# Joining paired operations across two PSUM banks in a fused attention and feed-forward kernel

## The reference

```
q, k, v = split(x @ Wqkv)                  # 16 heads of 64
q = l2norm(q) * qs; k = l2norm(k) * ks     # then a rotary embedding with scales
sim  = 8 * q k^T  in windows of 32 tokens, each looking at itself and the one before
sim  = where(mask, -max, sim)
attn = softmax(sim)
x    = x + (attn @ v) @ Wo
x    = x + (a * gelu(gate)) @ W2 + b2,   a, gate = split(layernorm(x) @ W1 + b1)
```

## Time and profile before

| | |
|---|---|
| time, median of 3 runs | 1455.85 us (1452.92 to 1457.2) |
| profiled execution, its own time | 1451.59 us |
| its span, first to last instruction | 1449.7 us |
| busy: PE matmul, PE weight load | 1357.1 us (94%), 1094.5 us (75%) |
| busy: DVE, ACT, POOL | 1294.6 (89%), 1266.6 (87%), 1184.0 us (82%) |
| chain that ended last, by engine | PE 47%, DVE 19%, issue 15%, ACT 6%, POOL 5% |
| a turn of the loop, around 740 us | 28.14 us |
| granted clock, mean | 0.986 |

### The profile page before, as it was taken

One profiled execution on the slowest core, in us unless ns is written; L12 is line 12 of the kernel. 1 busy time (PEld: TensorE's weight loads), 2 busy tenths in 40 slices (PEclk: granted clock), 3 DMA queues, 4 the chain that ended last, 5 costly groups with the idle time before them and its releaser, 6 DMA issues.

```text
span 1449.7 us, 76627 instructions
## 1 busy us (share of the span) xinstructions
PE 1357.1 (94%) x30176; PEld 1094.5 (75%) x30176; DVE 1294.6 (89%) x2400; ACT 1266.6 (87%) x2523; POOL 1184.0 (82%) x1162
## 2 busy tenths in 40 slices
PE   6589999999999999999999999999999999999985
PEld 4467777877777777777777777777777778777774
DVE  6688999999999999999999999999999999999973
ACT  6578999999999999999999999999999999899873
POOL 2687888888888888888888888888888888888860
PEclk9899999999999999999999999999999999999998
DMA  5221112131111222111122111113111112111111
GB/s 148 81 57 41 38 48 57 36 89 42 51 39 47 57 57 68 42 50 39 47 70 61 50 43 50 39 46 95 36 43 36 36 37 77 43 29 43 43 31 30
DMA packets 61752, 75.09 MB, mean 52 GB/s; under 512 B 8462, under 2 KB 35340, under 8 KB 61708
## 3 DMA queue, kind: packets, MB, share of 16 engines
q1 hardware_dynamic: 61708, 74.51, 18.8%
HBM read 18.90 MB, written 1.05 MB: 14 GB/s over the span
## 4 chain that ended last, share of the span: by engine, by line
PE 47%; DVE 19%; issue 15%; ACT 6%; POOL 5%; DVEq 2%; ACTq 0%; POOLq 0%
PE bank L1275 12%; PE bank L1178 6%; PE bank L1266 6%; DVE ss L906 5%; PE bank L1191 5%; PE bank L1179 4%; PE bank L1180 4%; DVE psum L943 4%; POOL u L444 3%; DVE u L913 3%; PE bank L1228 3%; PE bank L1311 3%; DVE t L922 3%; PE bank L1300 2%; ACT gate L714 2%
## 5 line engine op out<-in xcount | busy, mean ns | idle before, releaser
L444 POOL TENSOR_TENSOR u<-u,t 128x512 f32<-128x512 f32 x384 | 490.5, 1283 | 84.3 <-DVE t L922 68.5
L457 POOL TENSOR_TENSOR u<-u,rn 128x512 f32<-128x512 f32 x384 | 388.9, 1045 | 0.0
L628 ACT ACTIVATE sq<-bank 128x512 f32<-128x512 f32 x384 | 234.0, 610 | 64.0 <-PE bank L1180 62.0
L1178 PE MATMUL bank<-Wl,xsh 128*128 (+1 forms) x576 | 268.0, 465 | 15.4 <-POOL xsl L439 11.3
L463 POOL TENSOR_TENSOR P<-P,rs 128x512 f32<-128x512 f32 x192 | 196.6, 1045 | 95.0 <-DVE rs L948 95.0
L922 DVE TENSOR_TENSOR t<-bank,TS 128x512 f32<-128x512 f32 x384 | 258.7, 684 | 6.1 <-ACT sq L628 2.1
L906 DVE TENSOR_REDUCE ss<-sq 128x8 f32<-128x512 f32 x384 | 255.6, 676 | 6.4 <-issue 6.4
L913 DVE TENSOR_TENSOR u<-bank,TC 128x512 f32<-128x512 f32 x384 | 255.1, 675 | 1.3 <-ACT sq L628 1.3
L652 ACT COPY qkT<-bank 128x512 f32<-128x512 f32 x384 | 225.2, 603 | 13.5 <-PE bank L1191 6.4
L1179 PE MATMUL bank<-Wh,xsl 128*128 (+1 forms) x576 | 228.8, 397 | 0.0
L1180 PE MATMUL bank<-Wh,xsh 128*128 (+1 forms) x576 | 228.7, 397 | 0.0
(11 more groups left out here) (92 smaller groups left out, 2732.1 us busy)
## 6 DMA issues: line engine op xcount, KB each, us to landing
vs<-v SPq DMA_DIRECT2D x384, 128.0 KB, 2.3
Wraw<-in_L_ffn_Wqkv_dram SPq DMA_DIRECT2D x72, 117.5 KB, 2.1
WoS<-in_L_ffn_Wo_dram SPq DMA_DIRECT2D x6, 512.0 KB, 4.0
W1h<-Wh SPq DMA_DIRECT2D x6, 341.0 KB, 2.6
W1l<-Wl SPq DMA_DIRECT2D x6, 341.0 KB, 2.9
Wraw<-in_L_ffn_W_dram SPq DMA_DIRECT2D x12, 116.0 KB, 2.2
out_dram<-X SPq DMA_DIRECT2D x4, 256.0 KB, 2.7
W2S<-in_L_ffn_W_dram SPq DMA_DIRECT2D x6, 128.0 KB
```

What stands on the lines that cost most here:

```text
L444: nc.gpsimd.tensor_tensor(u[:, r, c], u[:, r, c], t2[:, r, c % 2], ALU.add).then_inc(add_done[c], 1)
L457: nc.gpsimd.tensor_tensor(by_head(u[:, r, c]), by_head(u[:, r, c]), spread(rn[:, r, HC * c:HC * c + HC], HC, DH), ALU.mult).then_inc(qk_re ...
L1178: nc.tensor.matmul(out, x[0], Wl[:, w], start=True, stop=False)
```

## The change

Where two instructions did the same to two banks, or to two halves of a tensor, one now does both. For every item `masks`, `v_out`, `exp`, `maxima`, `minus_maxima`, `row_sums` and `divide` are one instruction of 1024 elements a partition. The copies of turned heads are joined for k = 0 and 1 of both items (`all_heads_out(0)`), not for k = 2 and 3; the copies of turned `P` for item 0 alone (`all_p_out`). Each joined instruction has one semaphore instead of two. So that one instruction can address two banks, the banks are one tensor `PS`, and the rows of `BANK_USERS` are put in another order, so that the two banks of a joined step are neighbours (read backwards where the second lies lower); who shares a bank with whom stays as it was. The mask lies twice in the constants that are loaded at the start (9 * 128 columns for 7 * 128). The order of TensorE's steps is the same.

```diff
-        sc = sb("shape_constants", [128, 7 * 128])
+        sc = sb("shape_constants", [128, 9 * 128])
...
-        K = [bank(str(k)) for k in range(8)]
+        PS = es.enter_context(nc.psum_tensor("banks", [128, 8, 512], F32))
+        K = [PS[:, k] for k in range(8)]
...
+        HEADS_AT_ONCE, P_AT_ONCE = [[True, True], [False, False]], [True, False]
...
-                 "v": lambda k, r: [v_ready[k]],
-                 "turn_qk": lambda k, r: [qk_out[k]],
-                 "scores": lambda k, r: [sc_out[k]],
-                 "turn_p": lambda k, r: [PT_ready[k]],
+                 "v": lambda k, r: [v_ready],
+                 "turn_qk": lambda k, r: [qk_out[r][k - k % 2 if HEADS_AT_ONCE[k // 2][r] else k]],
+                 "scores": lambda k, r: [sc_out],
+                 "turn_p": lambda k, r: [PT_ready[r][0 if P_AT_ONCE[r] else k]],
...
+        def banks_of(kind, k=0, r=0):
+            b, b2 = (bank_place(kind, k + e, r)[0] for e in range(2))
+            return PS[:, b:b + 2] if b < b2 else PS[:, b2:b + 1][:, ::-1]
...
-                def divide(e, lag, r):
+                def divide(lag, r):
                     n = (it - lag) * 2 + r
                     pool.wait_ge(rs_done, n_(n) + 1)
-                    nc.gpsimd.tensor_tensor(P[:, r, e], P[:, r, e], spread(rs[:, r, e], 8, DH),
-                                            ALU.mult).then_inc(P_ready[e], 1)
+                    nc.gpsimd.tensor_tensor(item(P, r), item(P, r), spread(item(rs, r), 16, DH),
+                                            ALU.mult).then_inc(P_ready, 1)
...
-                def masks(e, lag, r):
-                    n = (it - lag) * 2 + r
-                    for readers, value in bank_left(it - lag, "scores", e, r):
+                def masks(lag, r):
+                    for readers, value in both_left(it - lag, "scores", 0, r):
                         act.wait_ge(readers, value)
-                    nc.scalar.copy(bank_of("scores", e, r)[:].rearrange("p (s t n) -> p s t n", s=2, t=2),
-                                   maskf.unsqueeze(2).broadcast_to([128, 2, 2, 128])).then_inc(seeded[e], 1)
+                    nc.scalar.copy(banks_of("scores", 0, r).rearrange("p e (s t n) -> p e s t n", s=2, t=2),
+                                   maskf.unsqueeze(3).broadcast_to([128, 2, 2, 2, 128])).then_inc(seeded, 1)
...
+                def all_heads_out(s, lag, r):
+                    pair = it - lag
+                    act.wait_ge(qk_turned[s], n_(pair * 2 + r) + 1)
+                    act.wait_ge(sc_full[s], n_(pair * 2 + r) - 1)
+                    nc.scalar.copy(qkT[:, r, s].rearrange("p w t (g i) -> p g (w t) i", g=2),
+                                   banks_of("turn_qk", 2 * s, r).rearrange("p g (k i) -> p g k i", i=64)
+                                   ).then_inc(qk_out[r][2 * s], 1)
...
                 if on(1):
-                    heads_out(0, 1, 0)
+                    all_heads_out(0, 1, 0)
                     square(1, 1, 1)
-                    heads_out(1, 1, 0)
                     heads_out(2, 1, 0)
...
                     square(2, 1, 1)
-                    masks(1, 1, 0)
-                    masks(0, 1, 0)
+                    masks(1, 0)
                     heads_out(3, 1, 0)
...
                     norms(1, 1)
-                    v_out(0, 1, 1)
+                    v_out(1, 1)
                 if on(0):
                     square(3, 0, 0)
-                if on(1):
-                    masks(1, 1, 1)
                 if splitting:
                     split_high()
                 if on(1):
-                    masks(0, 1, 1)
-                    v_out(1, 1, 1)
-                    exp(1, 1, 0)
-                    exp(0, 1, 0)
+                    masks(1, 1)
+                    exp(1, 0)
...
                     heads_out(3, 1, 1)
-                    heads_out(1, 1, 1)
+                    all_heads_out(0, 1, 1)
                 if on(2):
                     inverse_deviation(2)
-                if on(1):
-                    heads_out(0, 1, 1)
...
-                def minus_maxima(e, lag, r):
-                    n = (it - lag) * 2 + r
-                    dve.wait_ge(mx_done[e], n_(n) + 1)
+                def minus_maxima(lag, r):
+                    n = (it - lag) * 2 + r
+                    dve.wait_ge(mx_done, n_(n) + 1)
                     dve.wait_ge(P_turned, n_(n) - 1)
-                    nc.vector.tensor_tensor(P[:, r, e], by_head(bank_of("scores", e, r)[:], 8), spread(nm[:, r, e], 8, DH),
-                                            ALU.subtract).then_inc(sc_out[e], 1)
+                    nc.vector.tensor_tensor(P[:, r], heads_of_two(banks_of("scores", 0, r)),
+                                            nm[:, r].unsqueeze(3).broadcast_to([128, 2, 8, DH]),
+                                            ALU.subtract).then_inc(sc_out, 1)
...
                 if on(2):
                     residual(2)
-                if on(1):
-                    row_sums(0, 1, 0)
                 if on(0):
                     squares(1, 0, 0)
                 if on(1):
-                    row_sums(1, 1, 0)
+                    row_sums(1, 0)
                     reciprocals(1, 0)
...
-                    maxima(0, 1, 1)
-                    maxima(1, 1, 1)
-                    minus_maxima(1, 1, 1)
-                    minus_maxima(0, 1, 1)
+                    maxima(1, 1)
+                    minus_maxima(1, 1)
```

More of the change, by code:

```diff
@@ L261, in bank_left, with when_left, both_left, item @@
                 other, ok, orr, lag = users[at]
[L262 to L266, removed]
-            return []
+                away = users[place][3] + turns - lag
+                if not isinstance(pair, int) or 0 <= pair + away < PAIRS:
+                    return [(s, other in COUNTS_PAIRS, orr, away) for s in FREED[other](ok, orr)]
+            return []
+        def when_left(pair, users):
+            for s, per_pair, r, away in users:
+                if per_pair:
+                    yield s, n_(pair + away + (LAYER_PAIRS if s is h_ready else 0)) + 1
+                else:
+                    yield s, n_((pair + away) * 2 + r) + 1
+        def bank_left(pair, kind, k=0, r=0):
+            return when_left(pair, user_before(pair, kind, k, r))
+        def both_left(pair, kind, k, r):
+            first, second = user_before(pair, kind, k, r), user_before(pair, kind, k + 1, r)
+            return when_left(pair, first + [user for user in second if user not in first])
         def column(at, pair, per=1, k=0, rows=slice(0, 128)):
             return fc[rows, ds(pair // LAYER_PAIRS * per + (at + k), 1)]
+        def item(t, r):
+            if len(t.shape) == 5:
+                return t[:, r].rearrange("p e g c -> p (e g) c")
+            return t[:, r].rearrange("p e g -> p (e g)")
         def layer(pair):
@@ L674, in o_out, with all_p_out @@
+                def all_p_out(lag, r):
+                    pair = it - lag
+                    act.wait_ge(P_turned, n_(pair * 2 + r) + 1)
+                    act.wait_ge(pv_full, n_(pair * 2 + r) - 1)
+                    nc.scalar.copy(PT[:, r].rearrange("p e (t g i) -> p g (e t) i", g=2, i=64),
+                                   banks_of("turn_p", 0, r).rearrange("p g (k i) -> p g k i", i=64)
+                                   ).then_inc(PT_ready[r][0], 1)
                 def o_out(h, lag, r):
@@ L779, in step @@
                 if on(1):
[L780 to L781 removed]
+                    all_p_out(1, 0)
                 if on(0):
@@ L1003, in step @@
                     straight(2, 1, 1)
-                    maxima(0, 1, 0)
-                    maxima(1, 1, 0)
-                    minus_maxima(0, 1, 0)
-                    minus_maxima(1, 1, 0)
+                    maxima(1, 0)
+                    minus_maxima(1, 0)
                 if on(0):
@@ L1083, in cross_vT @@
                 arrived(pe, ctx_in, g)
-                nc.tensor.matmul(CROSS_B[g][:], wvT[:], whole(ctxS, g), start=True, stop=True).then_inc(c_vT, 1)
+                nc.tensor.matmul(CROSS_B[g], wvT[:], whole(ctxS, g), start=True, stop=True).then_inc(c_vT, 1)
             def cross_q(g):
                 pe.wait_ge(c_xTs, g + 1)
-                nc.tensor.matmul(CROSS_A[g][:], wqT[:], xhT4[g], start=True, stop=True).then_inc(c_q, 1)
+                nc.tensor.matmul(CROSS_A[g], wqT[:], xhT4[g], start=True, stop=True).then_inc(c_q, 1)
             def cross_v(g):
```

161 lines of the change are left out of this document (76 added, 85 removed).

## The result

The changed kernel takes 1489.44 us (median of 4, 1488.46 to 1494.15) against 1454.38 for the kernel before: 1.0253 times as long, with a 95% interval of 1.0213 to 1.0293. The forecast was 1482 within 1457 to 1497, slower. The profiled execution has a span of 1487.8 us, 38.1 more than before.

What follows compares the result with a forecast made beforehand. TensorE's fixed order and its three stops were taken as the bound. Terms of 0.46 + 0.20 + 0.10 − 0.08 − 0.07 = +0.61 us a turn, times 46, plus 1.0, gave 1485.0 us; forecast 1482, range 1457 to 1497.

Steps and rivals of the forecast that it cites:

- the chain to `xfl`: Item 1's joined heads delay `rstdx`, then `normal`, `xfl` and `up`: +0.10 us a turn, bounds 0 and 0.20.
- the heads of item 0: The joined copy ends later, so transposition `turn_qk(1, 1, 0)` starts later: +0.46 us a turn.
- What a join costs: Joined operations at 1.06 to 1.21 us, saving 0.02 to 0.07 each; whoever needs the first half waits 0.46 or 0.52 longer.
- the 0.08 to be given back: Joined exponential and v copies let ScalarE begin item 0's heads copy sooner: −0.08 us a turn, 0 to −0.14.
- the low bound: Item 0's heads: only +0.18 us a turn if just 0.06 must follow the copy, as outside the loop.
- The masks ahead of `xsh`: Joined masks stand before `xsh`, and TensorE waits for `xsl` behind it: −0.07 us a turn.
- Item 1's subtraction: Joined subtraction frees the bank later for `v_chunk(1, 0, 0)`: +0.20 us a turn, from +0.07 to +0.26.
- At nothing: Joins charged zero: item 1's exponential, row sums and division, v copies, others; slack or TensorE's existing stops were to hide them.
- stalls beyond the sum: Rival: late row sums push rotations, joined masks wait for `swapped(1, 0, 1)`; about 1.0 us a turn, 1500 us, chance 0.12.
- The load: The doubled mask adds 128 KB to the load TensorE awaits at the start: 1.0 us once, bounds 0 and 2.5.
- Little ends: Rival: queue work overlaps the heads' copy, so the turn grows only 0.04 to 0.1 us; 1458 to 1461, chance 0.14.
- faster: Rival: joins save their fixed cost, some 0.12 us each, and TensorE's three stops shrink; 1442 us, chance 0.10.

Runs made afterwards that it cites:

- e2: Changed kernel with the copies of item 1's first heads separate again; turn 28.58 us, 1.0138 times the kernel before.
- e9: Kernel before, no joins, with the wait met last put last where several stand in a row; turn 27.93 us, ratio 0.9941.
- e12: Changed kernel with the waits reordered so that the one met last comes last; turn 28.79 us, 1.0206 times the kernel before.
- e11: Changed kernel with item 1's exponential and row sums, item 0's masks and item 0's copy of v apart, other joins kept; turn 29.00 us, ratio 1.0259.
- e3: Changed kernel with item 1's subtraction in two instructions again, maxima still joined; turn 28.95 us, 1.0271 times the kernel before.
- e4: Changed kernel with both items' copies of first heads and item 1's subtraction apart, other joins kept; turn 28.55 us, ratio to before 1.0106.
- e6: Kernel of e4 with item 0's masks also in two instructions again; turn 28.18 us, 1.0004 times the kernel before.
- e8: Kernel of e4 with item 1's exponential and row sums, item 0's masks and item 0's copy of v also apart; turn 28.10 us, ratio 0.9981.
- e10: Kernel of e8 with the waits in the order of e9 and the mask loaded once; turn 27.81 us, 1439.93 us, ratio to before 0.9891.
- e1: Changed kernel with the copies of item 0's first heads separate again; turn 28.89 us, 1.0207 times the kernel before.
- e7: Kernel of e4 with item 0's copy of v also bank by bank; turn 28.54 us, 1.0121 times the kernel before.

## Why the prediction was right

**Direction and size.** Right: the joins shorten busy engines that were not the bound, and lengthen the releases that TensorE waits for. The sum was +0.61 a turn and the turn grew by 0.77; on the median 29.1 us were summed, 35 measured. That the sum came this close is in part luck: the chain to `xfl` was 0.25 too low, the heads of item 0 were 0.12 too high, and the last term agrees for another reason than the one given.

**What a join costs.** The duration was right within 0.03 us for both engines that had two widths to draw a slope from. GpSimd saved 0.14 a pair (2.05 to 1.906), more than a few hundredths, and nobody waited for it. The rule of the Trainium skill ("VectorE: DVE Perf Modes", section "The TRN2 errata — SBUF-src ops pay a fixed extra latency per instruction") gave an estimate of 0.14 us saved a join on ScalarE, from its figure for reads of PSUM. Of the joins that read PSUM, the trace shows 1.08 to 1.03 for heads and 1.08 to 1.02 for v, so 0.05 to 0.06; the masks (1.13 to 1.02) and the exponential (1.15 to 1.06), which read SBUF, save 0.11 and 0.09. All lie between the rows' guess and the estimate.

**The chain to `xfl`: right in mechanism, mis-sized.** The term was +0.10 and measured +0.35 (e2 gives all of it back). `rstdx` came even 0.11 sooner than I had it. But `normal` was taken to follow it by 0.04, and it follows by 0.39. The rows of the prediction had it already: `rstdx` ends at 732.42 and `normal` begins at 732.82, 0.40 later, while VectorE's instruction ahead of it is over at 732.75:

```profile
731.47 1.28 DVE L913 TENSOR_TENSOR u<-bank,TC 128x512 f32<-128x512 f32 x2
```

So `normal` hung on `rstdx` in the kernel before as well, with no slack, and what delays the one delays the other in full; the prediction took that distance for slack. Inside the loop another wait, the count and the operand's address stand behind this wait. After the loops `normal` follows by 0.18 in the kernel before (1407.96 + 0.42 to 1408.56, the timelines of ScalarE and VectorE):

```profile
1407.96 0.42 ACT L698 ACTIVATE rstdx<-lvx 128x256 f32<-128x256 f32 x1
```

```profile
1408.56 0.49 DVE L964 SCALAR_TENSOR_TENSOR bank<-bank,feature_columns,rstdx 128x256 f32<-128x256 f32 x1 [1.74 <-ACT rstdx L698]
```

The very same kind of gap I had priced for TensorE's transposition. I used it there and not here. This term alone is larger than the miss.

**The heads of item 0: right in mechanism, too dear.** +0.26 against +0.38 net. The copy runs 1.01 us here, so it is 0.38 longer and not 0.46, and the transposition follows by 0.24 (762.42 to 762.66) and not 0.34. Of the 0.08 to be given back only 0.02 was: the copy begins 0.12 behind the end of its transposition (761.29 to 761.41), where it began 0.14 behind, so ScalarE was not what was late. e9 and e12 show that the order of waits sets a part of the gap behind the copy; why it is shorter in the changed kernel without that edit was not tried, and in e11 it is 0.36 again (821.18 to 821.54). The 0.06 that the low bound was taken from runs to the weight load and the 0.34 to the matmul; that matmul begins at 1391.14, so like for like it is 0.09, and the sum is not touched.

**The masks ahead of `xsh`: right by luck.** The term was −0.07 and the stretch shrank by 0.05, but `xsh` begins no sooner: 22.51 after the residual and not 21.72, and 14.80 behind `up` and not 14.36. The stretch is shorter because the transposition at its start has been put off by more than `xsh` has.

**Item 1's subtraction: the size was right, and a part was missed.** The v product moved by 0.17 (0.20 foreseen). That the joined copy of v, too, would hold the next transposition at the same place was not seen: it stood among what costs nothing, on the ground that the waits view showed no stop there. The view of before can't show a stop that a longer release will make. In the sum the miss does not show, since the two fall on the same place (e3).

**At nothing.** The delay of the row sums was sized right (0.35, measured 0.35), and the division of item 1 does not hold TensorE, as foreseen. The delay was not followed down VectorE's own queue to the masks. The rival "stalls beyond the sum" had named exactly that chain, joined masks waiting for `swapped(1, 0, 1)`, and expected it on top. It exists (e4, e6), and in the changed kernel it costs nothing extra, because the heads' copy makes `xsh` just as late.

**The load.** The 1.0 us for it is not borne out. The wait for the constants grew by 0.1 us in the profile after, and e8 with the doubled mask starts sooner than e10 with the single one.

**The rivals.** "Little ends" is ruled out by the new wait for `qkT`; "faster" by the three stops, which grew from 39.8 to 53.7 us together. Its core is true in e8 and e10, where the joins that hold nobody up do make the kernel faster.

## What to carry to other kernels

Before two operations are joined, list who waits for the first half, in each queue, and who waits behind the second instruction; where one of them feeds the bound engine, the join costs up to the length of a half, against a saving of a tenth of a microsecond. Look for a second chain that ends at the same place before you add a loss or undo a cause: here three edits that each took away a real delay won next to nothing alone (e1, e3, e7). Where several waits stand in a row, put the one that is met last at the end.

## What was not expected of the hardware

Behind a wait that is met late inside a hardware loop, 0.24 to 0.40 us pass in these kernels until the next operation starts, on TensorE and on VectorE. Outside the loops, in the kernel before, it is 0.09 at the transposition and 0.18 at `normal`. Part of it hangs on the order of the waits in the row: putting the late one last took 0.09 to 0.24 us off each gap, and 0.24 a turn off the kernel before. What of the rest is the count, the operand's address or the loop itself was not tried.
